# Graph network kernel: a step's own gate products brought forward on its first side alone, with changes in the order of VectorE, ScalarE and GpSimd

## What is computed

```
for _ in range(5):
    s_in  = state @ in_W.T + in_b
    s_out = state @ out_W.T + out_b
    a_in  = A @ s_in
    a_out = A.T @ s_out
    a = concat(a_in, a_out, state)
    r = sigmoid(a @ r_W.T + r_b)
    z = sigmoid(a @ z_W.T + z_b)
    h = tanh(concat(a_in, a_out, r * state) @ h_W.T + h_b)
    state = (1 - z) * state + z * h
out = tanh(state @ o1_W.T + o1_b) @ o2_W.T + o2_b
result = layernorm(x + out)
```

## Time and profile before

| | |
|---|---|
| median of 3 runs | 657.39 us (656.48 to 657.84) |
| the profiled execution's own time | 657.65 us |
| its span | 655.9 us |
| TensorE matmuls busy | 638.1 us, 97% |
| VectorE busy | 524.4 us, 80% |
| ScalarE busy | 418.2 us, 64% |
| GpSimd busy | 68.1 us, 10% |

### The profile page before, as it was taken

The page is one execution under the profiler, slowest core; times in us unless marked ns, Lnnn a source line. Parts: engine busy times, 40 slices in busy tenths (PEclk is TensorE's granted clock), DMA queues, the critical chain, the costliest instruction groups (busy, mean ns, idle before and its releaser), DMA issues. The chain is left out here.

```text
span 655.9 us, 8678 instructions
## 1 busy us (share of the span) xinstructions
PE 638.1 (97%) x2860; PEld 525.3 (80%) x2860; DVE 524.4 (80%) x833; ACT 418.2 (64%) x562; POOL 68.1 (10%) x61
## 2 busy tenths in 40 slices
PE   8999999999999999999999999999999999999993
PEld 7888888887888788788888877888887888887883
DVE  4996889799578739987896998887689888746886
ACT  2774645478357726895665688575758966674645
POOL 0092025200500720000000000000000000000012
PEclk9999999999999999999999999999999999999998
DMA  8999657213200270324034223403342250213003
GB/s 290 332 360 239 169 179 195 42 46 49 101 1 32 58 196 37 67 63 161 33 131 66 92 63 66 160 32 128 58 134 55 42 193 1 96 65 129 1 0 132
DMA packets 111609, 70.40 MB, mean 107 GB/s; under 512 B 89424, under 2 KB 95696, under 8 KB 110544
## 3 DMA queue, kind: packets, MB, share of 16 engines
q1 hardware_dynamic: 103056, 68.84, 35.1%
q10 hardware_dynamic: 8512, 1.05, 1.1%
HBM read 47.85 MB, written 19.40 MB: 103 GB/s over the span
## 5 line engine op out<-in xcount | busy, mean ns | idle before, releaser
L1158 ACT ACTIVATE work<-work,bias 128x512 f32<-128x512 f32 x120 | 86.0, 723 | 125.2 <-DVE work L1679 124.6
L1679 DVE SCALAR_TENSOR_TENSOR work<-degree,deg_w,bank 128x512 f32<-128x512 uint16 x120 | 88.4, 744 | 28.1 <-PE bank L703 27.3
L1017 ACT ACTIVATE ring<-a 128x1024 fp32r<-128x1024 uint8 (+1 forms) x91 | 91.7, 1048 | 6.3 <-PE bank L822 3.1
L701 PE MATMUL bank<-u_c,fold 128*128 128x512 f32 x240 | 94.1, 392 | 1.6 <-DVE work L1679 1.5
L702 PE MATMUL bank<-u_c,fold 128*128 128x512 f32 x240 | 93.4, 389 | 0.0
L703 PE MATMUL bank<-u_c,fold 128*128 128x512 f32 x240 | 93.4, 389 | 0.0
L822 PE MATMUL bank<-ring,rows 128*128 128x512 f32 x384 | 90.8, 390 | 0.3 <-DVE ring L1452 0.3
L714 PE MATMUL bank<-ring,rows 128*128 128x512 f32 x384 | 88.6, 389 | 0.2 <-issue 0.2
L1050 ACT ACTIVATE ring<-sums,minus 128x1024 fp32r<-128x1024 uint8 x72 | 80.3, 1139 | 7.5 <-PE bank L822 6.5
L822 PEld LDWEIGHTS bank<-ring,rows 128*128 128x128 f32 x384 | 71.7, 188 | 16.5 <-DVE ring L1452 1.0
L714 PEld LDWEIGHTS bank<-ring,rows 128*128 128x128 f32 x384 | 72.0, 188 | 15.5 <-issue 0.6
(11 more groups left out here) (168 smaller groups left out, 1110.9 us busy)
## 6 DMA issues: line engine op xcount, KB each, us to landing
sums<-sums_dram SPq DMA_DIRECT2D x12, 768.0 KB, 5.0
stage<-in_adj_dram SPq DMA_DIRECT2D x15, 512.0 KB, 8.6
sums<-in_adj_dram SPq DMA_DIRECT2D x13, 512.0 KB, 6.4
turned_dram<-work SPq DMA_DIRECT2D x12, 512.0 KB, 2.6
rows<-turned_dram SPq DMA_DIRECT2D x192, 32.0 KB, 2.0
sums_dram<-sums SPq DMA_DIRECT2D x4, 768.0 KB, 3.5
l_dram<-rs_c SPq DMA_DIRECT2D x3, 1024.0 KB, 3.9
rs_c<-l_dram SPq DMA_DIRECT2D x3, 1024.0 KB, 4.9
```

The costliest lines, as they stand in the source:

```text
L701: nc.tensor.matmul(out_, wh, vh, start=first, stop=False)
L1017: nc.scalar.activation(out_, in_, ACT.Copy).then_inc(s, 1)
L1158: nc.scalar.activation(gates[:, g, e, :], gates[:, g, e, :], ACT.Tanh if g == H else ACT.Sigmoid, bias=bias[:, g, e:e + 1]).then_inc(gate_ ...
L1679: nc.vector.scalar_tensor_tensor(out=gates[:, g, e, :], in0=degree[:, c * CW:(c + 1) * CW], scalar=deg_w[:, g, e:e + 1], in1=g_bank[s % 3] ...
```

## The change

The diff:

```diff
--- before.py
+++ after.py
@@ -673,7 +673,7 @@
             pool.wait_ge(pair_stored, S_PAIR)
             pool.wait_ge(row_lo, row_count(1, (NC - 1, 1)))
             sum_blocks(1, range(6))
-            pool.wait_ge(state_new, S_TWO + 2 * TWO)
+            pool.wait_ge(mixed, mixed_at(1, 1, W5))
             pool.wait_ge(sums_kept[0], 16)
             pool.wait_ge(pair_used, used_at(1, 0, P3, 1))
             sum_blocks(2, range(6))
@@ -777,7 +777,8 @@
                             if p == NP - 1 and d == 0:
                                 last.then_inc(agg_done, 1)
                     last.then_inc(pair_used, 1)
-                own_ahead(t, 2 * side, range(OWN_AHEAD))
+                if side == 0:
+                    own_ahead(t, 0, range(OWN_AHEAD))
 
             def product_rows(product, part, p, jj):
 
@@ -802,7 +803,7 @@
 
                 pe.wait_ge(u_lo, t * S_TWO + side * 2 * TWO)
                 for n, (kind, p) in enumerate(ORDER):
-                    if n in OWN_AT:
+                    if side == 0 and n in OWN_AT:
                         own_ahead(t, 2 * side, OWN_AT[n])
                     tile = ring[:, n % RING]
                     if n in BY_ACT:
@@ -843,7 +844,7 @@
                 for s in range(2 * DB):
                     g, e = s // DB, s % DB
 
-                    if first or c % 2 or s >= OWN_AHEAD:
+                    if first or c or s >= OWN_AHEAD:
                         wait(pe, gate_read, t * S_GATE + c * GATE + s - 2)
                         own_part(g_bank[s % 3], g, e, st_c)
                     if last_step and (c, s) == (NPK, 1):
@@ -1236,7 +1237,7 @@
                     final_split(FINAL_AT[c, 2])
                 next_cast()
                 gate(t, c, 3)
-                if not ending:
+                if not ending and not half(t + (c == NC - 1)):
                     for e in range(DB):
                         split_state(*((t, 2) if c == 1 else (t + 1, 0)), e)
                 next_cast()
@@ -1308,6 +1309,8 @@
                     cast(t, side, k)
                 for k in range(12, 16):
                     cast(t, side, k)
+                    if k % 2 == 1:
+                        split_state(t, 2 * side, k // 2 - 6)
                 for k in range(16, 20):
                     if side == 0 and k < 18:
                         row_high(t, 3, k - 16)
@@ -1800,7 +1803,7 @@
                         split_state(t, c + 1, e)
                     for d in range(DB):
                         split_u(t, c + 1, d)
-                if c == NC - 1 and not last or c == 1 and not first:
+                if (c == NC - 1 and not last or c == 1 and not first) and not half(t + (c == NC - 1)):
                     for e in range(DB):
                         split_state(*((t, 2) if c == 1 else (t + 1, 0)), e)
                 if last and c == NC - 1:
@@ -1864,6 +1867,8 @@
                     row_low(t, 2, 1)
                 for _ in range(4):
                     test()
+                for e in range(DB):
+                    split_state(t, 2 * side, e)
                 if side == 0:
                     row_low(t, 3, 0)
                 test()
@@ -1892,21 +1897,15 @@
                     l_add(t, L1)
                     row_low(t, L11, 0)
                 cast(t, side, 0)
-                if side:
-                    test()
                 cast(t, side, 1)
                 if side == 0:
                     row_low(t, L1, 0)
+                cast(t, side, 2)
+                cast(t, side, 3)
+                if side == 0:
                     for h in range(2):
                         row_low(t, 1, h)
-                else:
-                    test()
-                    test()
-                cast(t, side, 2)
-                if side:
-                    test()
-                cast(t, side, 3)
-                for _ in range(4 if side else 2):
+                for _ in range(6 if side else 2):
                     test()
                 if side == 0:
                     l_add(t, L2)
@@ -1916,7 +1915,9 @@
                     l_add(t, L3)
                 cast(t, side, 4)
                 test()
+                test()
                 cast(t, side, 5)
+                test()
                 test()
                 if side == 0:
                     for k in (L22, L3, L4):
```

## The result

The changed kernel takes **650.05 us** (median of 4 runs, 649.49 to 650.49) where the kernel before, beside it on the same chip, takes 657.08 (4 runs, 656.48 to 657.84): 7.0 us less, ratio 0.9892 with the interval 0.9878 to 0.9907. The profiled execution's own time is 649.49, its span 647.7 (before 657.65 and 655.9).

The account below looks back on a forecast made before the run. TensorE's late starts, eight stalls, were taken to bound the kernel; 1.3 + 1.1 + 0.6 + 2.6 - 0.3 = 5.3 us off the median of 657.39 forecast 652.2 us, range 650.8 to 655.3 (the forecast's own 650.8 to 653.6).

Parts of the forecast that it names:

- Edit 2, 1.3 taken: Step 1, first side: without VectorE's state splits two ScalarE casts start earlier; gain 1.3 us (0.9 to 1.8).
- a little more: Step 1, first side: stall remaining beyond 0.3 us, where casts of 0.95 us follow matmuls of 0.91.
- Edit 3, 1.1 taken: Step 1, second side: two VectorE casts take 2.35 us, not 4.29, and the stall goes; 1.1 us (0 to 1.2).
- The second rival: Step 1, second side: collisions move with GpSimd, the 1.1 is given back and more; 653.3 to 654.3; chance 0.08.
- Edit 4, 0.6 taken: Step 3, first side: cast 2 ends 1.2 us earlier and its stall goes; gain 0.6 us (0 to 0.8).
- Edit 1, 2.6 taken: Last chunks of steps 1 to 4: VectorE's backlog shrinks and four gate stalls go; gain 2.6 us (0 to 2.7).
- The first rival: Gates: VectorE's backlog stays, however early gate 0 comes, and the 2.6 is missing; 654.8 us; chance 0.13.
- The charge of 0.3 for the second sides: Second sides of steps 2 to 4: casts losing own products as cover may start late; cost 0.3 us (-0.2 to 1.2).
- a dry ring: Second sides, steps 2 to 4, tiles 9 to 19: up to 4.08 us lost each; chance 0.05 slower, 0.05 655.6 to 658.7.
- a new stall at tile 14: Step 1's DMA row or the swapped casts' stall at tile 14: 1 to 1.5 us less gain, 653.3 to 653.7; chance 0.07.
- the eight cost 6.1: TensorE's eight listed stalls: brackets of 3.8 us plus 8 x 0.29 make 6.1 us, nearly all the change can win.
- all terms at their best: Sum of every term's best end: 1.8 + 1.2 + 0.8 + 2.7 + 0.2 = 6.7 us, giving 650.7 us.

Follow-up runs that it names:

- Edit 2: Step 1's state splits moved from behind gate 3 into the aggregate; alone against the kernel before: 656.08 us, ratio 0.9993.
- Edit 3: GpSimd's third call waits for mix W5 instead of the new state; alone against the kernel before: 655.64 us, ratio 0.9986.
- Edit 4: VectorE's order in the aggregates of steps 2 to 4 changed, tests no longer between early casts; alone against the kernel before: 655.74 us, ratio 0.9985.
- edit 1: Own products brought forward on the first side only, not both; alone against the kernel before: 656.98 us, ratio 1.0002.
- all but edit 1: The changed kernel with own products ahead on both sides again: 653.21 us, ratio 0.9937 against the kernel before.
- the repeat: The changed kernel itself measured again beside the kernel before: 649.77 us against 656.86, ratio 0.9891.
- mix C12: The changed kernel with GpSimd's third call moved later, behind mix C12 of step 1's second side: 657.05 us, ratio 0.9997 against the kernel before.

## Why the prediction was right, and where it was wrong

- **What bounds it: right.** TensorE's starts bound the kernel. With the stalls gone the eight sides fell by 6.70 us and the time by 7.03.
- **Edit 2, 1.3 taken: 1.20 measured** (61.65 to 60.45), 1.16 alone. The two casts were to start at 149.1 and 150.65; in the old count of time they start at 149.1 and 150.7 (148.36 and 149.88 plus the 0.78 by which the side now begins earlier). The stall left, of 0.17, is within "a little more".
- **Edit 3, 1.1 taken: 1.27 measured**, alone and in company. GpSimd's start, forecast near 220.6, came at 218.61, which is 220.59 with the 1.98 us by which the side now begins earlier. The second rival, collisions that eat the gain, fell: they came, but 3.66 of the 8.02 us of cover were left. One link was off: SyncE is not busy until the sums are there. Its 16 loads are issued by 226.67 and the store goes at 228.05, when GpSimd's sixth operation has ended; nothing behind it waited for those 1.4 us.
- **Edit 4, 0.6 taken: 0.55 alone**, the right size, but edit 1 is a second cause. The side lost 0.82 in the end, but edit 1 alone gives 0.55 of that, since it brings the row sooner, and from all but edit 1 to the changed kernel the side still loses 0.38. The stall's own size is that of one execution: 0.30 here, 0.61 and 0.93 in the two others with a stall. Its second side, costed at nothing, was right as the sum of the change, but as a price for that edit it misled: left out, the same edit costs 4.3 us.
- **Edit 1, 2.6 taken: 2.8 measured.** The four sides with a gate stall give 0.68 (1.95 less edit 3's 1.27), 0.63, 0.63 (0.87 less edit 4's 0.24) and 0.88, and chunk 3's gate 2 came 1.8 us sooner against 1.5. The first rival, a backlog that stays, fell. Gate 5 comes 1.4 us behind its product, against the 1.3 or less named as the sign. What the prediction lacked is edit 1's gain in the first sides, another 0.5.
- **The charge of 0.3 for the second sides: 0.** Step 2's second side has ScalarE's casts 6 to 9 done by 332.20 (four from 328.32 in 3.88 us), with tile 9 wanted at 324.62 + 9 x 0.907 = 332.78: 0.6 us of room, as forecast. There was no stall, so nothing was due. The third and fourth rivals, a dry ring and a new stall at tile 14, show nowhere in the changed kernel.

**The step that failed** is the one that set the ceiling: "the eight cost 6.1. That is nearly all the change can win". The eight sides had 7.16 us above what they take without any stall (459.38 less 452.68, plus the 0.17 + 0.29 still there). The missing 1.0 us was in starts late by a tenth or less, which the list of stalls leaves out and the busy figure hides; the prediction put it at nothing. Nearly all of it lies in the first sides of steps 2, 3 and 4 and the second of step 3 (0.22, 0.23, 0.14, 0.28). The runs show which edits take it: step 3's second side falls by 0.24 with edit 4 alone, and the first sides of steps 2 and 4 by all of it with edit 1 alone, by 0.12 and 0.10 with edit 4 alone. The section on edit 1 looked for its effect on the second sides and never on the first ones. The account of the miss in the sides: 5.3 forecast, + 0.3 for the charge not due, + 0.1 for terms rounded down (5.6 against 5.69 for the stalls that went), + 1.0 for losses under the list's threshold = 6.7. The "all terms at their best" of 6.7 happened to be that number, but for the wrong reason, and it left the range no room for the 0.3 between the sides and the medians (7.03, and 7.09 in the repeat). Another 0.3 of the distance to the forecast is the base: the forecast was taken from the median of 657.39 then at hand, and with one more run it is 657.08. The 0.3 between sides and medians lie outside the eight sides. There, over the 13 executions profiled, the first product comes at 21.1 to 22.2 us and 11.95 to 12.64 pass between the last matmul's start and the end of the own time. What sets those I have not settled. The time behind the last matmul's start is 11.95 to 12.25 in seven of the eight kernels with edit 1 (12.61 in the one with mix C12) and 12.38 to 12.64 in the five without; whether edit 1 is the cause is not shown.

The mechanism stood for each stall that was priced. What was wrong was the size, through the late starts and edit 1's reach into the first sides, and the range, whose low end was built from the same incomplete list.

## What to carry to other kernels

Before adding up stalls, measure the ceiling: the length of a stage less its count of matmuls times their spacing. Where the same stage runs several times, the copy that shows no stall in the list can still be tenths above the floor. Where an edit moves an engine's list forward, follow it into the next stage as well. And cost an edit in the company that it will have: own products moved away were worth 0.0 alone and 3.2 us once the tests no longer stood between the casts, and the reorder of the tests was worth 4.3 us only beside them.

## What the runs showed of the hardware that I had not expected

**The clock can fall on short pauses.** The prediction put no cost on the clock, since no stall of the kernel before was longer than 1 us. In two kernels the same pair of stalls occurs in step 2's second side. With edit 1 alone (0.98 and 0.54 us) the granted clock stays at the upper level; with the tests between the casts (0.99 and 0.52 us) it falls to 0.50, that is 1.2 GHz, behind the second. Windows of TensorE, edit 1 alone:

```profile
337.00:340.00 3.00, 2.02 (x10) 1.00 0.05 9
340.00:343.00 3.00, 2.46 (x11) 1.00 0.40 63
```

The tests between the casts:

```profile
337.00:339.00 2.00, 1.48 (x5) 1.00 0.36 55
339.00:340.00 1.00, 1.00 (x4) 0.53 0.37 57
...
341.00:342.00 1.00, 1.00 (x4) 0.50 0.43 67
342.00:343.00 1.00, 1.00 (x5) 0.77 0.43 66
```

That side takes 61.73 against 60.17: 1.6 us for the clock on 2.1 for the stalls. In the GpSimd kernel (mix C12) the pause was 4.18 us, and the clock fell too:

```profile
250.00:255.00 5.00, 0.82 (x4) 0.87 0.98 330
255.00:260.00 5.00, 5.00 (x13) 0.50 0.37 146
```

Of that side's extra 7.2 us some 2.7 are the clock (7.2 - 4.18 - 0.29). The trace doesn't say why one pair of short stalls took the clock and its twin did not. In the other eleven profiled executions the granted clock stays at 1.00 from step 1 to the end of step 4, with single stalls of up to 1.06 us among them.

The unprofiled executions have only a mean clock each. With the tests between the casts the profiled one has 0.992 and is the slowest of five (655.54); the four others have 0.995 or 0.996 and lie at 653.62 to 654.87. With edit 1 alone one of eleven has 0.991, and it is the slowest (658.89, the median is 656.98); the others have 0.994 to 0.996. With mix C12 all eleven have 0.990 to 0.992, so there the long pause took the clock each time. So a short stall seems to have a second price that comes in some executions only (1.6 us in the one that was traced; the one of 0.991 was not), and a forecast that opens stalls, as the dry ring does, should carry it in the range. The Trainium skill (TensorE: Matmul & The Clock Gate, "What's actually happening") says that a gate sets the clock by how busy the array has been recently. That both falls come behind or inside pauses agrees with it; why the twin kept its clock, it does not tell.

**VectorE and GpSimd by turns.** While GpSimd's sums run, VectorE's operations with two inputs from SBUF stretch, and those with one input from a bank of TensorE's output do not: the tests go from 0.7 to 1.32 each, the splits from 0.65 to 1.6, the split of u from 0.69 to 1.38, but the two operations at 230.53 and 231.14 take 0.69 and 0.68. The Trainium skill (SBUF — State Buffer, "SBUF: two separate sides") names this an exclusive lock for a whole instruction, between GpSimd and a VectorE operation with two SBUF inputs; the trace agrees. What it costs is decided by what stands behind those operations: 1.27 us in front of a cast that TensorE waits for, nothing in front of the idle time.
